# Six blocks of the projection phase made into one, and the next sequence's input and q weights requested at the head of the attention block

## The chip, the cores and the metric

The kernel runs on the 8 cores of one Trainium2 chip. Each core takes two of the 16 sequences and works on its own; no core waits for another. The time is device time in microseconds (us) of the slowest core. A profile is one execution, recorded on the slowest core, with the span and granted TensorE clock of all eight. PE is TensorE, DVE is VectorE, ACT is ScalarE, POOL is GpSimd, SP is SyncE.

## The reference, cut to what matters

One transformer layer over x of (16, 2048, 1024) in float32: attention, a LayerNorm, a feed-forward part with quantized activations and weights and a depthwise convolution, and a LayerNorm.

```
def _L0_attn_ref(x, w_qkv, w_fc, b_fc, gamma, beta):
    qkv = jnp.einsum('bsd,ed->bse', x, w_qkv)
    q, k, v = jnp.split(qkv, 3, axis=-1)
    att = jax.nn.softmax(jnp.einsum('bqd,bkd->bqk', q, k) * scaling, axis=-1)
    y = jnp.einsum('bqk,bvd->bqd', att, v)
    y = jnp.einsum('bqd,ed->bqe', y, w_fc) + b_fc
    h = x + y
    return layernorm(h) * gamma + beta
...
x = _layernorm(x + _L0_attn_ref(...))
x = _layernorm(x + _L0_ffn_ref(x, w1, conv_w, conv_b, w2))
```

The einsum 'bqk,bvd->bqd' sums att over k and v over its own positions, so that each row of y is the row sum of att times the sum of all rows of v. The kernel makes use of this: it needs q, k, the row sums of the softmax, and one row, the sum of x over the positions times the v weights times the fc weights.

## The kernel before

The program is a row of blocks. A helper class, PB, collects each engine's instructions and waits in lists; run() writes them out as one block, and the next block begins on every engine when all engines have ended the one before (the waits show such a block end as PEq L65). Inside a block each engine runs its own list in order, and semaphores order the engines among each other: mm counts PE's groups, vv DVE's, ssm ACT's, dG the DMAs of POOL, dS and dSb those of SP. After each of its DMA instructions POOL also runs a drain.

First come constants (P0) and the means of the feed-forward weights (W0), until 209 us. Then, for each of the two sequences:

- A0: POOL requests the feature-major input, eight DMAs of 128 x 2048 elements from float32 into the bfloat16 tile xf (L432), and the q weights, eight DMAs of 128 x 1024 elements into wbuf (wload, L411). It waits for all of them, and the block ends.
- A1: PE multiplies in 32 groups of eight matmuls (L445), alternating between two PSUM banks; DVE evicts each group into qf (L453).
- A2kl: POOL loads the k weights into the same wbuf, and the block ends when they are there.
- A2k: the same 32 groups with the k weights, evicted into kf (L469).
- A2v: DVE sums xf over the positions, eight reductions of 2048 elements (L479); PE multiplies the sums with the v weights, which SP brings in eight pieces through a buffer of two (L491, L497); the row goes to DRAM and back as columns (L508, L512).
- A2w: the same with the fc weights (L529, L535), and the row is spread to all partitions in wrowbc (L550).
- A3: sixteen query tiles. For each, SP loads a residual tile into xres (L581), PE forms 128 x 2048 scores in 32 matmuls (L589), DVE takes maxima (L598), ACT the exponentials and their sums (L607), and emit_epilogue adds, normalizes twice, quantizes and has ACT store x1, a scale, and the quantized tile (L291 to L398). The epilogue of a tile is emitted inside the next tile's turn. Of DVE's work over 1024 elements there, L330, L365, L384, L387, L393 and L627 read one tile each.
- A3drain: every engine waits for all stores and loads of A3.

The tile xf is allocated for A0 to A2v alone and is given back before A3; wbuf is allocated throughout. In A3 POOL has nothing to do, and neither xf nor wbuf is used.

After both sequences come the feed-forward half: w1 quantized, the first matmul with the convolution (F1), w2 quantized, and the second matmul (F2). Nothing of it is touched by the change.

Of the kernel before, what the change touches and what calls it, by code (L numbers as in the profile page):

```python
# [8 lines left out]
BF16 = mybir.dt.bfloat16  # L9
# [72 lines left out]
def build_program(cfg: Cfg, debug=False):  # L82
    nc = bass.Bass("TRN2", target_bir_lowering=False)
    S, D, H, DC, HC = cfg.S, cfg.D, cfg.H, cfg.DC, cfg.HC
    T, G, KB, KBW = cfg.T, cfg.G, cfg.KB, cfg.KBW
    T1, T2, ST = cfg.T1, cfg.T2, cfg.ST
    NGRP, NQT, NSEQ = cfg.NGRP, cfg.NQT, cfg.NSEQ
# [10 lines left out]
    x_fm = din("x_fm", (NSEQ, D, S))  # L98
    wqT = din("wqT", (D, D))
# [68 lines left out]
    dG = Sem(E(nc.semaphore("dG")))  # L168
    dO = Sem(E(nc.semaphore("dO")))
    mm = Sem(E(nc.semaphore("mm")))  # L170
    vv = Sem(E(nc.semaphore("vv")))
# [3 lines left out]
    p = PB(nc, "P0")  # L175
    for dst, srcd in ((ident, ident_d), (identf, identf_d), (esel, esel_d),
                      (onescol, ones_d), (c128, c128_d)):
        p.op("sync", lambda s, dst=dst, srcd=srcd: s.dma_start(
            out=dst[:], in_=srcd.ap()), inc=dS, k=16)
    p.op("sync", lambda s: s.dma_start(  # L180
        out=gammaBC[:], in_=_ap(gamma_d.tensor, 0, [[0, 128], [1, D]])),
        inc=dS, k=16)
    p.op("sync", lambda s: s.dma_start(
        out=betaBC[:], in_=_ap(beta_d.tensor, 0, [[0, 128], [1, D]])),
        inc=dS, k=16)
    p.op("sync", lambda s: s.dma_start(
        out=bfcBC[:], in_=_ap(bfc_d.tensor, 0, [[0, 128], [1, D]])),
        inc=dS, k=16)
    for c in range(HC):
        p.op("sync", lambda s, c=c: s.dma_start(  # L190
            out=cwcol[:, 3 * c:3 * c + 3], in_=cw_d[c * 128:(c + 1) * 128, :]),
            inc=dS, k=16)
    for c in range(HC):
        p.op("sync", lambda s, c=c: s.dma_start(
            out=cbcol[:, c:c + 1], in_=cb_d[c * 128:(c + 1) * 128, :]),
            inc=dS, k=16)
# [5 lines left out]
    with nc.sbuf_tensor("wstage", [128, H], F32) as wstage, \  # L202
         nc.sbuf_tensor("wstage2", [128, H], F32) as wstage2, \
         nc.sbuf_tensor("wabs", [128, H], F32) as wabs:
        p = PB(nc, "W0")
# [5 lines left out]
        for i, (src, width) in enumerate(chunks):  # L211
# [7 lines left out]
            if i >= 1:  # L219
                p.wait("scalar", vv, vv.n)  # L220
            p.op("scalar", lambda sc, stage=stage, width=width: sc.activation(
                out=wabs[:, 0:width], in_=stage[:, 0:width], func=AF.Abs), inc=ssm)
            p.wait("vector", ssm, ssm.n)
            p.op("vector", lambda v, i=i, width=width: v.reduce_sum(
                out=colsb[:, i:i + 1], in_=wabs[:, 0:width], axis=AX.X), inc=vv)
        p.op("vector", lambda v: v.reduce_sum(
            out=cols[:, 0:1], in_=colsb[:, 0:DC], axis=AX.X))
        p.op("vector", lambda v: v.reduce_sum(
            out=cols[:, 1:2], in_=colsb[:, DC:DC + HC], axis=AX.X), inc=vv)
# [8 lines left out]
            out=wsmat[0:1, 2:3], in0=wsmat[0:1, 0:1], scalar1=1.0 / (D * H),  # L238
            scalar2=1e-5, op0=ALU.mult, op1=ALU.max))
        p.op("vector", lambda v: v.tensor_scalar(  # L240
            out=wsmat[0:1, 3:4], in0=wsmat[0:1, 1:2], scalar1=1.0 / (D * H),
# [6 lines left out]
            out=wsmat[0:1, 8:9], in0=wsmat[0:1, 6:7], scalar1=-1.0, scalar2=None,  # L248
            op0=ALU.mult))
        p.op("vector", lambda v: v.tensor_scalar(  # L250
            out=wsmat[0:1, 9:10], in0=wsmat[0:1, 7:8], scalar1=-1.0, scalar2=None,
            op0=ALU.mult), inc=vv)
        p.wait("tensor", vv, vv.n)
        for j, cell in enumerate((4, 5, 8, 9)):
# [5 lines left out]
             inc=vv)  # L260
# [141 lines left out]
    attn_stack = ExitStack()  # L402
# [6 lines left out]
    def wload(p, src):  # L409
        for dc in range(DC):  # L410
            p.op("gpsimd", lambda g, dc=dc, src=src: g.dma_start(  # L411
                out=wbuf[:, dc * D:(dc + 1) * D],
                in_=src[dc * 128:(dc + 1) * 128, :]), inc=dG, k=16)

    def mm_evac(p, items, emit_group, emit_evac, banks):
# [3 lines left out]
        for i, it in enumerate(items):  # L419
# [5 lines left out]
            emit_evac(p, it, banks[i % nb])  # L425
            assert vv.n == evbase + i + 1

    for s_i in range(NSEQ):
        with nc.sbuf_tensor(f"xf{s_i}", [128, DC * S], BF16) as xf:
            p = PB(nc, f"A0_{s_i}")  # L430
            for dc in range(DC):
                p.op("gpsimd", lambda g, dc=dc: g.dma_start(  # L432
                    out=xf[:, dc * S:(dc + 1) * S],
                    in_=x_fm[s_i, dc * 128:(dc + 1) * 128, :]), inc=dG, k=16)
            wload(p, wqT)
            p.wait("gpsimd", dG, dG.n)
            p.run()

            q_items = [(cb, ec) for cb in range(S // KBW) for ec in range(DC)]

# [14 lines left out]
                    in0=bank[:, 0:KBW], scalar1=cfg.QSCALE, scalar2=None,  # L455
                    op0=ALU.mult), inc=vv)

            p = PB(nc, f"A1_{s_i}")
            mm_evac(p, q_items, q_group, q_evac, [ps_a, ps_b])
            p.run()  # L460

            p = PB(nc, f"A2kl_{s_i}")
            wload(p, wkT)
            p.wait("gpsimd", dG, dG.n)
            p.run()

            def k_evac(p, it, bank):
                cb, ec = it
# [1 line left out]
                    out=kf[:, ec * S + cb * KBW: ec * S + (cb + 1) * KBW],  # L470
                    in_=bank[:, 0:KBW]), inc=vv)

            p = PB(nc, f"A2k_{s_i}")
            mm_evac(p, q_items, q_group, k_evac, [ps_a, ps_b])
            p.run()

            p = PB(nc, f"A2v_{s_i}")
            for dc in range(DC):
                p.op("vector", lambda v, dc=dc: v.reduce_sum(  # L479
                    out=colsb[:, 32 + dc:33 + dc], in_=xf[:, dc * S:(dc + 1) * S],  # L480
# [5 lines left out]
            for dc in range(DC):  # L486
                sem = dS if dc % 2 == 0 else dSb
                if dc >= 2:
# [3 lines left out]
                    out=wf32[:, (dc % 2) * D:(dc % 2 + 1) * D],  # L492
                    in_=wvT[dc * 128:(dc + 1) * 128, :]), inc=sem, k=16)
# [8 lines left out]
            for h in range(NDH):  # L502
                bank = ps_c if h == 0 else ps_d
                p.op("vector", lambda v, h=h, bank=bank: v.tensor_copy(
                    out=vrow[0:1, h * DH:(h + 1) * DH], in_=bank[0:1, 0:DH]),
                    inc=(vv if h == NDH - 1 else None))
            p.wait("sync", vv, vv.n)
            p.op("sync", lambda s: s.dma_start(out=vrow_d, in_=vrow[0:1, :]),  # L508
                 inc=dS, k=16)
            p.wait("sync", dS, dS.n)  # L510
            for dc in range(DC):
                p.op("sync", lambda s, dc=dc: s.dma_start(  # L512
                    out=colsb[:, 40 + dc:41 + dc],
                    in_=_ap(vrow_d.tensor, dc * 128, [[1, 128], [1, 1]])),
                    inc=dS, k=16)
            p.run()

        p = PB(nc, f"A2w_{s_i}")
        p.wait("sync", dS, dS.n)
        p.wait("sync", dSb, dSb.n)  # L520
        p.wait("tensor", dS, dS.n)
# [2 lines left out]
        for dc in range(DC):  # L524
            sem = dS if dc % 2 == 0 else dSb
            if dc >= 2:
# [3 lines left out]
                out=wf32[:, (dc % 2) * D:(dc % 2 + 1) * D],  # L530
                in_=wfcT[dc * 128:(dc + 1) * 128, :]), inc=sem, k=16)
# [7 lines left out]
        for h in range(NDH):  # L539
# [3 lines left out]
                out=rowbuf[0:1, 0:DH], in_=bank[0:1, 0:DH]), inc=vv)  # L543
# [7 lines left out]
                out=wrowbc[:, h * DH:(h + 1) * DH], in_=ps_s[0][:, 0:DH]),  # L551
                inc=vv)
# [15 lines left out]
        if True:  # L568
            if True:
                p = PB(nc, f"A3_{s_i}")  # L570
                dO_bases = {0: dO.n, 1: dOb.n}
                exp_ev = {}
                mm_at = {}
                epi_q = {}
                for qt in range(NGRP * NQT):
# [3 lines left out]
                    if qt >= 2:  # L579
                        p.wait("sync", vv, ev_h2_list[qt - 2])  # L580
                    p.op("sync", lambda s, row0=row0, qt=qt: s.dma_start(  # L581
                        out=xres[:, (qt % 2) * D:(qt % 2 + 1) * D],
                        in_=x_tm[row0:row0 + 128, :]), inc=ldsem, k=16)
# [579 lines left out]
```

How the kernel before makes its waits and increments, by code:

```python
        def cl(e, fn=fn, tgt=tgt, drain=drain):  # L52
            ins = fn(e)
            if tgt is not None:
                ins.then_inc(*tgt)
            if drain:
                e.drain()
# [3 lines left out]
    def wait(self, eng, sem, val):  # L61
        self.items[eng].append(lambda e, h=sem.h, v=val: e.wait_ge(h, v))
```

## Time and profile before

| | us |
|---|---|
| median of 2 runs | 4921.29 (4916.14 and 4926.43) |
| the profiled execution | 4925.33 |
| its span, slowest core (core 1) | 4923.6 |
| spans of the other cores | 4901.7 to 4923.3 |
| A0 to A2w, first sequence | 209 to 522 |
| A3 and drain, first sequence | 522 to 997 |
| A0 to A2w, second sequence | 997 to 1313 |
| A3 and drain, second sequence | 1313 to 1784 |
| feed-forward half | 1784 to 4923 |

The span runs from the first to the last instruction of a core; the time of an execution has a little around it. Busy time of an engine is the time in which it executes; DMA instructions of POOL are counted as busy while they are issued (about 0.5 us each), the transfers themselves are not. A row of the order of time gives the start and the length in us, the engine, the line, what is written and read, how many instructions are merged, and in brackets how long the engine was idle before and what ended that.

### The profile page before, as it was taken

The page shows a single profiled execution, that of the slowest core. Times are in us where ns is not written, and L with a number is a line of the kernel's source. Part 1 is how long each engine was busy: PE and PEld are TensorE (multiplying, and loading weights), DVE is VectorE, ACT ScalarE, POOL GpSimd, SP SyncE. Part 2 cuts the span into 40 slices and gives each one's busy share as a digit, 9 for nine tenths or more (in the row PEclk, how much of TensorE's full clock was granted, in tenths as well). Part 3 has the DMA queues.
Part 4 walks back from the last instruction along what each step waited for, and adds up shares of the span by engine and source line. Part 5 has one row for each costly group of instructions (what it writes and reads, how often), then busy time and mean ns, then how long its engine had stood idle before and what let it go on. Part 6 is the DMA issues. An engine that isn't in the chain of part 4 may idle for free. (4 is left out here: it accounts for less than half of the span.)

```text
span 4923.6 us, 35107 instructions; the slowest of 8 cores (4901.7 to 4923.6 us)
## 1 busy us (share of the span) xinstructions
PE 1830.1 (37%) x8500; PEld 922.5 (19%) x8500; DVE 3281.7 (67%) x4522; ACT 967.7 (20%) x1773; POOL 25.7 (1%) x52
## 2 busy tenths in 40 slices
PE   0046533127533303423323323233333333106999
PEld 0022111013111102211212211122111121003444
DVE  3313488802388876888888888888888888874333
ACT  2200122100022202222223222232222322100111
POOL 0000000000000000000000000000000000000000
PEclk9998766658766656666566666566565766558999
DMA  5521111131211131000000000000000000035543
GB/s 165 150 36 46 58 52 45 45 51 18 77 54 43 53 131 38 1 23 23 23 23 16 7 24 23 23 13 11 23 23 24 21 3 18 17 120 166 163 145 107
DMA packets 189264, 258.95 MB, mean 53 GB/s; under 512 B 63490, under 2 KB 131330, under 8 KB 187012
## 3 DMA queue, kind: packets, MB, share of 16 engines
q1 hardware_dynamic: 163716, 197.95, 13.4%
q10 hardware_dynamic: 18432, 41.97, 2.2%
q0 software_dynamic: 6912, 16.78, 2.1%
q14 instruction: 134, 1.10, 0.1%
q8 instruction: 70, 1.15, 0.1%
HBM read 188.47 MB, written 75.52 MB: 54 GB/s over the span
## 5 line engine op out<-in xcount | busy, mean ns | idle before, releaser
L868 PE MATMUL ps_a<-xqF,tw 128*128 128x258 bf16 (+1 forms) x1024 | 219.3, 386 | 1002.5 <-DVE ubuf L879 777.0
L892 ACT ACTIVATE vt<-ubuf,cbcol,cwcol 128x256 f32<-128x256 f32 x512 | 307.7, 601 | 919.2 <-DVE ubuf L879 889.0
L589 PE MATMUL ps_s<-kf,qf 128*128 128x512 bf16 x1024 | 294.9, 459 | 507.9 <-ACT disc L607 505.6
L868 PE MATMUL ps_s<-xqF,tw 128*128 128x258 bf16 (+1 forms) x2048 | 315.2, 308 | 50.5 <-DVE ubuf L879 47.6
L868 PEld LDWEIGHTS ps_a<-xqF,tw 128*128 128x128 bf16 x1024 | 124.9, 130 | 1080.4 <-issue 1037.9
L816 DVE TENSOR_TENSOR accb<-accb,rbuf 128x2048 bf16<-128x2048 bf16 x256 | 313.6, 1225 | 19.7 <-issue 0.9
L756 DVE SCALAR_TENSOR_TENSOR vt<-ubuf,cwcol,vt 128x256 f32<-128x256 f32 x512 | 248.3, 485 | 84.5 <-issue 55.2
L763 DVE SCALAR_TENSOR_TENSOR vt<-ubuf,cwcol,vt 128x256 f32<-128x256 f32 x512 | 248.3, 485 | 40.4 <-issue 2.6
L1031 PE MATMUL ps_c<-tw,hq 128*128 128x512 bf16 x512 | 195.4, 382 | 200.9 <-DMA hq<-hqs 200.9
L771 ACT ACTIVATE ubuf<-vt 128x256 f32<-128x256 f32 x512 | 213.7, 417 | 269.6 <-DVE vt L763 252.7
L915 PE MATMUL ps_c<-identf,maxM 128*128 128x128 f32 x64 | 19.1, 454 | 644.3 <-DVE maxM L908 644.3
L908 DVE TENSOR_REDUCE maxM<-ubuf 128x256 f32<-128x8192 f32 x16 | 247.5, 15467 | 9.9 <-ACT ubuf L771 9.9
L794 ACT ACTIVATE iqq<-zscr,c 128x2048 int32<-128x2048 f32 x64 | 128.1, 2002 | 604.1 <-DVE zscr L783 604.1
L589 PEld LDWEIGHTS ps_s<-kf,qf 128*128 128x128 bf16 x1024 | 114.6, 114 | 688.9 <-issue 615.6
L445 PE MATMUL ps_a<-xf,wbuf 128*128 128x512 bf16 x512 | 127.7, 395 | 302.8 <-PEq L65 302.8
L868 PEld LDWEIGHTS ps_s<-xqF,tw 128*128 128x128 bf16 x2048 | 209.6, 109 | 161.7 <-issue 114.7
L868 PE MATMUL ps_b<-xqF,tw 128*128 128x258 bf16 (+1 forms) x1024 | 216.3, 383 | 10.3 <-DVE ubuf L879 8.7
L1040 PE MATMUL ps_d<-tw,hq 128*128 128x512 bf16 x512 | 195.3, 381 | 0.0
L1031 PE MATMUL ps_s<-tw,hq 128*128 128x512 bf16 x512 | 194.0, 379 | 0.0
L1040 PE MATMUL ps_s<-tw,hq 128*128 128x512 bf16 x512 | 194.0, 379 | 0.0
L813 DVE TENSOR_SCALAR rbuf<-dsb 128x2048 bf16<-128x2048 bf16 x256 | 177.7, 694 | 20.0 <-issue 0.4
L607 ACT ACTIVATE disc<-ps_s,colsb 128x512 f32<-128x512 f32 x128 | 88.0, 687 | 409.0 <-DVE colsb L601 402.3
(137 smaller groups left out, 3041.0 us busy)
## 6 DMA issues: line engine op xcount, KB each, us to landing
hqs<-hqst SPq DMA_DIRECT2D x16, 2048.0 KB, 8.9
wstage<-w1T SPq DMA_DIRECT2D x8, 2048.0 KB, 10.3
wstage<-w2T SPq DMA_DIRECT2D x32, 512.0 KB, 4.0
xres<-x_tm SPq DMA_DIRECT2D x32, 512.0 KB, 3.4
x1s<-x1t ACTq DMA_DIRECT2D x32, 512.0 KB, 5.7
qstage<-w1T SPq DMA_DIRECT2D x8, 2048.0 KB, 8.7
qstage<-w2T SPq DMA_DIRECT2D x32, 512.0 KB, 3.3
xres<-x1s SPq DMA_DIRECT2D x32, 512.0 KB, 8.1
```

What stands on the lines that cost most here:

```text
L589: t.matmul(ps_s[kb][:, 0:KBW], qf[:, dc * S + qcol: dc * S + qcol + 128], kf[:, dc * S + kb * KBW: dc * S + (kb + 1) * KBW], start=(dc == ...
L756: v.scalar_tensor_tensor(out=vt2[:, cpar * T1W2:cpar * T1W2 + T1], in0=ubuf[:, hc * T1W2:hc * T1W2 + T1], scalar=cwcol[:, 3 * hc:3 * hc + ...
L763: v.scalar_tensor_tensor(out=vt1[:, cq * T1W2:cq * T1W2 + T1], in0=ubuf[:, hc * T1W2 + 2:hc * T1W2 + 2 + T1], scalar=cwcol[:, 3 * hc + 2:3 ...
L771: p.op("scalar", lambda sc, hc=hc, cq=cq: sc.activation(out=ubuf[:, hc * T1W2 + 1:hc * T1W2 + 1 + T1], in_=vt1[:, cq * T1W2:cq * T1W2 + T1 ...
L794: p.op("scalar", lambda sc, FD=FD: sc.activation(out=iqq[:, 0:FD], in_=zscr[:, 0:FD], func=AF.Identity, bias=c128[:, 0:1], scale=1.0), inc ...
L813: p.op("vector", lambda v, FD=FD, thr=thr: v.tensor_scalar(out=rbuf[:, 0:FD], in0=dsb[:, 0:FD], scalar1=thr, scalar2=None, op0=ALU.is_ge))
L816: p.op("vector", lambda v, FD=FD: v.tensor_tensor(out=accb[:, 0:FD], in0=accb[:, 0:FD], in1=rbuf[:, 0:FD], op=ALU.add))
L868: lo=lo, hi=hi, w0=w0, W=W: t.matmul(bank[:, 0:W], tw[:, dc * H + hc * 128: dc * H + hc * 128 + 128], xqF[:, (par * DC + dc) * WW + (lo - w0):
L892: p.op("scalar", lambda sc, hc=hc: sc.activation(out=vt1[:, (hc % 4) * T1W2:(hc % 4) * T1W2 + T1], in_=ubuf[:, hc * T1W2 + 1:hc * T1W2 + 1 ...
L908: p.op("vector", lambda v: v.reduce_max(out=maxM[:, 0:T1], in_=_ap(ubuf, 1, [[HC * T1W2, 128], [1, T1], [T1W2, HC]]), axis=AX.X, apply_abs ...
L1031: banks=banks: t.matmul(banks[0][:, 0:DH], hq2[:, slot + hc * T1 + sq * 128: slot + hc * T1 + sq * 128 + 128], tw[:, hc * D + 0:hc * D + D ...
L1040: banks=banks: t.matmul(banks[1][:, 0:DH], hq2[:, slot + hc * T1 + sq * 128: slot + hc * T1 + sq * 128 + 128], tw[:, hc * D + DH:hc * D + ...
```

## The change

- xf becomes one tile for both sequences, allocated for the whole attention half.
- The sixteen DMA instructions of A0 move into a function, emit_A0, which remembers the semaphore's count in dGq. For sequence 0 it is called at the head of the projection block; for sequence 1 it is called at the head of A3 of sequence 0.
- A0, A1, A2kl, A2k, A2v and A2w, six blocks, become one, APRO. In place of the five block ends between them stand waits: POOL and PE wait for the load of A0 (dGq), POOL waits for the last q matmul before it loads the k weights, and PE waits for these and for the last q eviction.

```
--- before.py
+++ after.py
@@ -425,16 +425,24 @@
             emit_evac(p, it, banks[i % nb])
             assert vv.n == evbase + i + 1
 
+    xf = attn_stack.enter_context(nc.sbuf_tensor("xfb", [128, DC * S], BF16))
+    dGq = {}
+
+    def emit_A0(p, s_i):
+        for dc in range(DC):
+            p.op("gpsimd", lambda g, dc=dc, s_i=s_i: g.dma_start(
+                out=xf[:, dc * S:(dc + 1) * S],
+                in_=x_fm[s_i, dc * 128:(dc + 1) * 128, :]), inc=dG, k=16)
+        wload(p, wqT)
+        dGq[s_i] = dG.n
+
     for s_i in range(NSEQ):
-        with nc.sbuf_tensor(f"xf{s_i}", [128, DC * S], BF16) as xf:
-            p = PB(nc, f"A0_{s_i}")
-            for dc in range(DC):
-                p.op("gpsimd", lambda g, dc=dc: g.dma_start(
-                    out=xf[:, dc * S:(dc + 1) * S],
-                    in_=x_fm[s_i, dc * 128:(dc + 1) * 128, :]), inc=dG, k=16)
-            wload(p, wqT)
-            p.wait("gpsimd", dG, dG.n)
-            p.run()
+        if True:
+            p = PB(nc, f"APRO_{s_i}")
+            if s_i not in dGq:
+                emit_A0(p, s_i)
+            p.wait("gpsimd", dG, dGq[s_i])
+            p.wait("tensor", dG, dGq[s_i])
 
             q_items = [(cb, ec) for cb in range(S // KBW) for ec in range(DC)]
 
@@ -455,14 +463,12 @@
                     in0=bank[:, 0:KBW], scalar1=cfg.QSCALE, scalar2=None,
                     op0=ALU.mult), inc=vv)
 
-            p = PB(nc, f"A1_{s_i}")
             mm_evac(p, q_items, q_group, q_evac, [ps_a, ps_b])
-            p.run()
-
-            p = PB(nc, f"A2kl_{s_i}")
+
+            p.wait("gpsimd", mm, mm.n)
             wload(p, wkT)
-            p.wait("gpsimd", dG, dG.n)
-            p.run()
+            p.wait("tensor", dG, dG.n)
+            p.wait("tensor", vv, vv.n)
 
             def k_evac(p, it, bank):
                 cb, ec = it
@@ -470,11 +476,8 @@
                     out=kf[:, ec * S + cb * KBW: ec * S + (cb + 1) * KBW],
                     in_=bank[:, 0:KBW]), inc=vv)
 
-            p = PB(nc, f"A2k_{s_i}")
             mm_evac(p, q_items, q_group, k_evac, [ps_a, ps_b])
-            p.run()
-
-            p = PB(nc, f"A2v_{s_i}")
+
             for dc in range(DC):
                 p.op("vector", lambda v, dc=dc: v.reduce_sum(
                     out=colsb[:, 32 + dc:33 + dc], in_=xf[:, dc * S:(dc + 1) * S],
@@ -513,9 +516,7 @@
                     out=colsb[:, 40 + dc:41 + dc],
                     in_=_ap(vrow_d.tensor, dc * 128, [[1, 128], [1, 1]])),
                     inc=dS, k=16)
-            p.run()
-
-        p = PB(nc, f"A2w_{s_i}")
+
         p.wait("sync", dS, dS.n)
         p.wait("sync", dSb, dSb.n)
         p.wait("tensor", dS, dS.n)
@@ -568,6 +569,8 @@
         if True:
             if True:
                 p = PB(nc, f"A3_{s_i}")
+                if s_i + 1 < NSEQ:
+                    emit_A0(p, s_i + 1)
                 dO_bases = {0: dO.n, 1: dOb.n}
                 exp_ev = {}
                 mm_at = {}
```

## Rows read from the trace of the kernel before

**Rows 1.** the page, busy time of each engine and DVE over 40 slices

```profile
PE 1830.1 (37%) x8500; PEld 922.5 (19%) x8500; DVE 3281.7 (67%) x4522; ACT 967.7 (20%) x1773; POOL 25.7 (1%) x52
...
DVE  3313488802388876888888888888888888874333
```

**Rows 2.** spans and granted clock of the two slowest cores

```profile
core 1: 4923.6 us, clock 0.696
...
core 6: 4923.3 us, clock 0.701
```

**Rows 3.** core 1 by stretch: length, busy (count) by engine, clock, DMA

```profile
209.00:287.00 78.00, 0.22 (x1) 0.14 (x2) 0.00 (x0) 0.00 (x0) 8.58 (x16) 1.00 0.49 81
...
438.00:522.00 84.00, 37.28 (x69) 5.75 (x70) 22.39 (x14) 0.00 (x0) 0.00 (x0) 0.77 0.32 100
522.00:997.00 475.00, 150.44 (x512) 58.03 (x512) 355.42 (x576) 100.89 (x257) 0.00 (x0) 0.63 0.13 45
997.00:1079.00 82.00, 0.27 (x1) 0.14 (x2) 0.00 (x0) 0.00 (x0) 8.45 (x16) 0.50 0.48 77
```

**Rows 4.** order of time, core 1, first A3 to second A1

```profile
983.14 0.34 ACTq L398 DMA_DIRECT2D xqs<-xqt  x1
997.17 0.53 POOL L432 DMA_DIRECT2D xf<-x_fm  x1 [621.75 <-PEq L65]
...
1074.78 0.53 POOL L411 DMA_DIRECT2D wbuf<-wqT  x1 [3.59 <-issue]
...
1078.73 3.57 PE L445 MATMUL ps_a<-xf,wbuf 128*128 128x512 bf16 x8 [156.48 <-PEq L65]
```

**Rows 5.** the same two points on core 6

```profile
997.75 0.53 POOL L432 DMA_DIRECT2D xf<-x_fm  x1 [617.59 <-PEq L65]
...
1077.90 3.52 PE L445 MATMUL ps_a<-xf,wbuf 128*128 128x512 bf16 x8 [154.95 <-PEq L65]
```

**Rows 6.** order of time, core 1, block ends, first sequence

```profile
282.76 0.53 POOL L411 DMA_DIRECT2D wbuf<-wqT  x1 [3.46 <-issue]
...
286.78 0.58 PE L445 MATMUL ps_a<-xf,wbuf 128*128 128x512 bf16 x1 [78.57 <-PEq L65]
...
343.07 1.89 PE L445 MATMUL ps_b<-xf,wbuf 128*128 128x512 bf16 x8
...
346.52 0.53 POOL L411 DMA_DIRECT2D wbuf<-wkT  x1 [63.23 <-PEq L65]
...
374.89 0.53 POOL L411 DMA_DIRECT2D wbuf<-wkT  x1 [3.55 <-issue]
...
378.83 3.57 PE L445 MATMUL ps_a<-xf,wbuf 128*128 128x512 bf16 x8 [33.87 <-PEq L65]
...
437.17 0.69 DVE L469 CAST kf<-ps_b 128x512 bf16<-128x512 f32 x1 [1.03 <-PE ps_b L445]
438.25 4.64 DVE L479 TENSOR_REDUCE colsb<-xf 128x1 f32<-128x2048 bf16 x2 [0.39 <-PEq L65]
```

**Rows 7.** SyncE's own waits, first 2600 us: total, times, longest

```profile
SPq L62 <- DMA colsb<-vrow_d: 3.4, 2, 2.1
```

**Rows 8.** DMA issues and queue share while the second load runs

```profile
q0 software_dynamic: 2304, 6.29, 47.8%
...
xf<-x_fm POOLq DMA_DIRECT2D x8, 512.0 KB, 5.7
wbuf<-wqT POOLq DMA_DIRECT2D x8, 256.0 KB, 3.5
```

**Rows 9.** DMA issues in the first A3, the residual load

```profile
xres<-x_tm SPq DMA_DIRECT2D x16, 512.0 KB, 3.4
```

**Rows 10.** groups of instructions, core 1, 560 to 960 us, two of DVE's six

```profile
L330 DVE TENSOR_SCALAR ln1t<-atile,cols 128x1024 f32<-128x1024 f32 x15 | 12.2, 813 | 10.1 <-ACT cols L315 10.1
...
L627 DVE TENSOR_SCALAR atile<-wrowbc,colsb 128x1024 f32<-128x1024 f32 x14 | 10.5, 753 | 1.1
```

**Rows 11.** waits of core 1, 560 to 960 us: total, times, longest

```profile
DVE x1t L365 <- ACT cols L359: 11.1, 15, 0.7
```

## The prediction

> **What bounds the kernel now.** I read the page first. VectorE (DVE) is busy for 67% of the span and TensorE (PE) for 37% [rows 1], but the average hides stages in which neither works. The line of forty slices shows them: DVE falls to 1 in the third slice and to 0 and 2 in the ninth and tenth (a slice is 123 us). So the next view is the table by stretch for core 1 [rows 3]. From 209 to 287 us, and again from 997 to 1079 us, PE is busy for less than 0.3 us, DVE and ScalarE for nothing; the only work is sixteen GpSimd (POOL) DMA instructions, with the DMA engines 48 to 49% busy. These are the blocks A0_0 and A0_1, which fetch the feature-major input and the q weights of a sequence. Between them lies A3_0, 522 to 997 us: DVE 355 of 475 us busy, POOL idle, DMA engines 13% busy. DVE sets the pace there: its own waits are short (0.7 us at the longest before L365 [rows 11]), and PE needs only 150 of the 475 us. The chain of work through the attention half is therefore load, q projection, load, k projection, a serial piece (438 to 522 us), A3, and the same again; what lies on it counts in full, because each block ends when all its engines have ended.
>
> The order of time puts the edges on it [rows 4]. The first A3 issues its last store at 983.14; a drain block waits for it; POOL issues the first transfer of the second load at 997.17, the last of its sixteen at 1074.78, and PE starts the second q projection at 1078.73. The second load costs core 1 1078.73 − 997.17 = 81.6 us.
>
> **The change, part by part.**
>
> *The second load moves into A3_0.* Removed from the path: 81.6 us on core 1 and 1077.90 − 997.75 = 80.15 us on core 6 [rows 5]. The time is that of the slowest core, and these two stand at 4923.6 and 4923.3 us [rows 2], so what counts is 4923.6 − 81.6 = 4842.0 and 4923.3 − 80.15 = 4843.15: core 6 becomes the slower, and the gain of this part is 4923.6 − 4843.15 = 80.45 us. The drain block before it stays, and so does the wait of 14 us for the last store.
>
> All sixteen DMA instructions move. They stand at the head of POOL's queue in A3_0, which has no other work, and wait for nothing: the readers of the input tile and of the weights ended before the previous block did. SyncE's and ScalarE's queues are not touched. The cover is 475 us for 81.6 us of loading, a factor of 5.8. The load runs at the start of A3_0, beside about 81.6 / 475 × 16 = 2.75, so three, query tiles.
>
> What it takes from them: first, DMA. The load uses 47.8% of the sixteen engines [rows 8] and A3 uses 13% [rows 3]; the sum is 61%. A residual tile lands in 3.4 us now [rows 9] and is issued about a tile (475 / 16 = 29.7 us) ahead of its use; even if a whole 5.7 us transfer of the load stood before it [rows 8], it would be in time. Cost nothing; without that lead it would be 5.7 us for each of three tiles. Second, DVE and POOL at the same time, which no stretch of before shows: wherever POOL works, DVE is idle. Per tile DVE has six instructions over 1024 elements that run in 0.7 to 0.8 us, more than one element in each nanosecond (L330, L365, L384, L387, L393, L627; two of them in [rows 10]). If POOL can hold something that these need, the bound from below is nothing, since each kind may pass untouched, and a gain is excluded because they do the same work. The bound from above is one POOL instruction of 0.53 us [rows 4] for each of 6 × 3 = 18 instructions, 9.5 us. I take 1 us, near the lower end, because POOL is busy for 8.5 of the 82 us [rows 3], about a tenth of the time, and a tenth of 9.5 us is 1.
>
> In the other direction those six instructions fill about 6 × 0.75 = 4.5 us of a 29.7 us tile, 15%. Were POOL locked out for all of them, the load would need 81.6 / 0.85 = 96 us instead of 81.6, still far inside 475. The Trainium skill (SBUF — State Buffer, "Summary: rules for kernel authors") warns against exactly such an overlap: descriptor generation for GpSimd's DMAs is starved while DVE runs its two-port modes, and it would have these DMAs issued from another queue. Its example, about 620 ns alone against 3100 ns overlapped, is a factor of 5; an estimate by it is a load of 5 × 81.6 = 408 us, which A3_0 would still cover. No run here shows that yet.
>
> *Six blocks of a sequence become one.* Where the blocks ended [rows 6], first sequence: the last q matmul ends at 343.07 + 1.89 = 344.96 and POOL starts the k weights at 346.52, a gap of 1.56 us which held the last eviction and the block's end. Now POOL waits for the matmul alone; I leave 0.3 us for the semaphore and take 1.26. The last k weight is issued at 374.89 and lands after 3.5 us (the row of the same transfers in [rows 8]), at 378.39; PE starts at 378.83: 0.44, of which 0.4 saved. The last k eviction ends at 437.86 and the row sums start at 438.25: 0.39, of which 0.32 saved. The q projection starts at 286.78, its last weight lands at 282.76 + 3.5 = 286.26: 0.4 saved, in the first sequence only (in the second that block's end went with the load). The end of A2v saves nothing: SyncE waits there 1.7 us each time for the column transfers to land [rows 7], and it still does. Sum: 2.38 in the first sequence and 1.98 in the second, 4.4 us. The bounds are 0 (other waits take it all) and twice that, 8.8.
>
> *What stays.* The k weights are still loaded behind the last q matmul, since both use one buffer. POOL's wait has only those eight DMAs behind it, and PE waits for them: 378.83 − 346.52 = 32.3 us of idle PE per sequence is not touched. PE's added wait for the evictions is over long before.
>
> *What comes early.* In the one block SyncE's first two loads of the v weights are issued at its start, beside the first input transfers in the first sequence. They are 512 KB each, like a residual tile's 3.4 us. The bound is 6.8 us, below is nothing; the load's transfers leave the DMA engines half idle [rows 3], so I take 1 us. In the second sequence they run beside matmuls, at no cost.
>
> *Sum.* 80.45 + 4.4 − 1 − 1 = 82.85 us. The profiled execution took 4925.3 us, 1.7 more than its span; the median of the runs is 4921.3, 4.0 below it. So 4925.3 − 82.85 = 4842.5 by the profiled execution, and 4838.5 by the median: 1.7% less. Within 2% (4822.9 to 5019.7 us), about what a measurement of this kernel can tell from no change, this counts as the same.
>
> **The rivals.**
>
> *DVE is held up by the load.* For: nothing in the trace excludes it. Against: POOL's short busy time. At the upper bound above, 8.5 us more than I took: 4847 us.
>
> *The load outlasts A3_0.* POOL's transfers would have to take over 5.8 times as long; at a factor of 7, 571 − 475 = 96 us would be left, and PE would start as late as before: 4838.5 + 80.45, about 4919 us, or with a few us less than 96, in between. Against: the six instructions fill only 15% of a tile.
>
> *Slower than before: POOL and DVE block each other through all of A3_0.* If the load is stretched over the whole stage, all 6 × 16 = 96 such DVE instructions meet it, and each may wait for POOL. From 82.85 / 96 = 0.86 us each the gain is gone; at 1.0 us, 4838.5 + 96 = 4934 us. Over 2% slower needs (82.85 + 98.4) / 96 = 1.9 us each. Against: 0.86 us is more than a whole POOL instruction.
>
> *More than the sum.* For over 2% faster the change must bring 98.4 us, 15.6 more than the sum. The block ends would have to hold four and a half times the 4.4 us that I read. The rows exclude it for this core; only another core or run could.
>
> *It does not do what it says.* If the load in A3_0 had to wait for something until the stage ends, 4.4 us would remain: about 4918 us. I see no such wait.
>
> **How the numbers follow.** The forecast has 0.76, with its own range of 4830 to 4846: 4.4 us more from block ends below, 5.8 us of early v loads above, and 2 to 4 us for other executions. DVE held up has 0.13, the load outlasting the stage 0.02, slower than before 0.02, more than the sum 0.04, no effect 0.03. The range is 4826 to 4852: it takes in the forecast and the first rival with 5 us around them, since the two times of before lie 10 us apart, and leaves out the other four, 0.11. Over 2% faster: 0.04. Over 2% slower: 0.01, half of the slower rival. Within 2%: 0.95.
>
> **What would show it.** In the profile after, POOL's sixteen instructions should stand within about 100 us from the start of A3_0, and the second q projection should start within 1 us of the drain's end. A3_0 should stay 475 us long, to 1 or 2 us; L330 and L627 should keep 813 and 753 ns. If A3_0 is longer by near 10 us, DVE was held up, and these two lines tell it. If POOL's transfers stand 20 us apart or more, it was starved. If the gap from the last q matmul to POOL is still 1.5 us, the block ends cost nothing. The forecast is wrong if another core had a much shorter second load than core 6 and a span near 4923, or if A3_0 pays for the load in a way that no row of before shows.

## The result

| | before | after |
|---|---|---|
| median of all executions, us | 4944.46 (10) | 4868.71 (12) |
| lowest, us | 4916.14 | 4830.39 |
| ratio | 1 | 0.9832, interval [0.9785, 0.988] |
| profiled execution, us | 4925.33 | 4868.29 |

The change takes 1.7% off the time, the share that the prediction gave (4838.5 / 4921.3 = 0.983); the interval reaches to both sides of 2%. The median of 4868.71 us lies 17 us above the range, though, and so does the first profiled execution. Executions of both kernels differ in the TensorE clock that is granted to pairs of cores (0 and 1, 2 and 3, and so on), and the ratio and its interval leave out those in which this makes one die over 1% slower. In two later series the changed kernel's median was 4863.67 (4 executions) and 4847.13 (6), beside 4931.56 and 4929.44 for the kernel before.

The spans and granted clocks of all cores of two profiled executions of the changed kernel, the first (4868.3 us) and one of the second series (4842.0 us):

```profile
core 0: 4839.6 us, clock 0.704
...
core 2: 4866.8 us, clock 0.696
core 3: 4862.2 us, clock 0.697
...
core 6: 4823.5 us, clock 0.706
...
core 0: 4830.5 us, clock 0.708
...
core 2: 4835.8 us, clock 0.705
core 3: 4840.5 us, clock 0.704
...
core 6: 4827.1 us, clock 0.705
```

In the first, cores 2 and 3 are 27 and 23 us later than core 0; their granted clock is 0.696 and 0.697 where that of the others is 0.703 or more. In the second no core stands out. The second is the one to hold against [rows 2]. Its page, busy time and the line of slices:

```profile
PE 1823.0 (38%) x8500; PEld 920.6 (19%) x8500; DVE 3281.8 (68%) x4522; ACT 967.6 (20%) x1773; POOL 26.1 (1%) x52
...
DVE  3313488823588767888888888888888888873334
```

Beside [rows 1] the counts of instructions are the same and the busy times of PE and DVE differ by 0.4% at most, and the second hole is narrower: DVE's ninth to eleventh slices were 0, 2 and 3 and are now 2, 3 and 5, and what is left of it are the projections and the serial piece, in which DVE has little to do. Order of time of core 3 there, from the last store of the first A3 to the second q projection (compare [rows 4]):

```profile
982.54 0.34 ACTq L398 DMA_DIRECT2D xqs<-xqt  x1
...
993.27 0.80 SPq L494 DMA_DIRECT2D wf<-wvT  x2
...
993.36 3.57 PE L453 MATMUL ps_a<-xfb,wbuf 128*128 128x512 bf16 x8 [71.75 <-PEq L65]
```

PE starts 10.8 us after the last store is issued, where it was 95.6 us on core 1 before (1078.73 − 983.14); the store lands at 992.57, so what is left is the drain's wait for it and the block ends.

Where the time went, stretch by stretch: means over the eight cores, read from the order of time of each core of the profiled executions, in us. The columns are two executions of the kernel before and two of the changed one.

| stretch | before | before, again | after | after, again | predicted difference |
|---|---|---|---|---|---|
| first load's start to first q eviction | 81.3 | 82.2 | 83.6 | 84.2 | +1 − 0.4 |
| its last weight landed to first q matmul (in the row above) | 0.50 | 0.50 | 0.14 | 0.14 | −0.4 |
| last q eviction's start to first k weight, first sequence | 1.45 | 1.45 | 0.43 | 0.43 | −1.26 |
| last k weight landed to first k matmul, first sequence | 0.51 | 0.51 | 0.25 | 0.25 | −0.4 |
| last k eviction's end to row sums | 0.38 | 0.38 | 0.09 | 0.09 | −0.32 |
| A3_0, DVE's first maximum to its last tile | 450.4 | 450.6 | 450.6 | 450.3 | +1 |
| A3_0's last tile to second q eviction | 94.8 | 94.1 | 13.5 | 12.9 | −80.45 |
| second load's first to sixteenth transfer | 75.5 | 75.6 | 110.1 | 115.6 | hidden |

From the start of the first load to the end of the second A3's last tile the cores take 1556.0 and 1555.6 us before and 1473.0 us after, again: 82.8 us less. (In the first execution of the changed kernel it is 1477.3 us; cores 0 and 1 had a lower clock in the second projections, as shown below.)

### The profile page after: what moved, and what is told of

It is laid out like the page before. It is cut to its first block and busy times, and to the rows that moved or that the text cites. A ratio compares the mean times of both kernels' runs of the same rounds, so it can differ in the third digit from the quotient of the medians.

```text
span 4866.8 us, 35003 instructions; the slowest of 8 cores (4823.5 to 4866.8 us)
## 1 busy us (share of the span) xinstructions
PE 1856.7 (38%) x8500; PEld 928.4 (19%) x8500; DVE 3281.8 (67%) x4522; ACT 967.6 (20%) x1773; POOL 25.8 (1%) x52
## 5 line engine op out<-in xcount | busy, mean ns | idle before, releaser
L871 PE MATMUL ps_s<-xqF,tw 128*128 128x258 bf16 (+1 forms) x2048 | 315.2, 308 | 55.4 <-DVE ubuf L882 52.7
L759 DVE SCALAR_TENSOR_TENSOR vt<-ubuf,cwcol,vt 128x256 f32<-128x256 f32 x512 | 248.3, 485 | 84.2 <-issue 55.2
L453 PE MATMUL ps_a<-xfb,wbuf 128*128 128x512 bf16 x512 | 127.4, 394 | 220.8 <-DMA wbuf<-wqT 80.7
L1043 PE MATMUL ps_s<-tw,hq 128*128 128x512 bf16 x512 | 202.6, 396 | 0.0
L1034 PE MATMUL ps_s<-tw,hq 128*128 128x512 bf16 x512 | 202.6, 396 | 0.0
```

The lines of the kernel that those rows point to most:

```text
L759: v.scalar_tensor_tensor(out=vt2[:, cpar * T1W2:cpar * T1W2 + T1], in0=ubuf[:, hc * T1W2:hc * T1W2 + T1], scalar=cwcol[:, 3 * hc:3 * hc + ...
L871: lo=lo, hi=hi, w0=w0, W=W: t.matmul(bank[:, 0:W], tw[:, dc * H + hc * 128: dc * H + hc * 128 + 128], xqF[:, (par * DC + dc) * WW + (lo - w0):
L1034: banks=banks: t.matmul(banks[0][:, 0:DH], hq2[:, slot + hc * T1 + sq * 128: slot + hc * T1 + sq * 128 + 128], tw[:, hc * D + 0:hc * D + D ...
L1043: banks=banks: t.matmul(banks[1][:, 0:DH], hq2[:, slot + hc * T1 + sq * 128: slot + hc * T1 + sq * 128 + 128], tw[:, hc * D + DH:hc * D + ...
```

## The experiments

### The kernels once more

No edit. Each execution comes with the clock and span of every core.

> The kernel before, unchanged, against itself. It is there for the executions: each lists its time and the granted clock of every core. Theory (the lower clock comes with or without the change): the ratio to the kernel before is 1.00 within 0.5%, and of its executions some stand near 4916 to 4926 us and others 35 to 60 us above these, the latter with one pair of cores whose mean granted clock is lower by 0.005 or more. Rival (the change itself brings the lower clock): all its executions stand within 10 us of 4920.

Measured: ratio to the kernel before 0.9995 [0.995, 1.004]. Six of its ten executions were at 4925 to 4961 us and four at 4989 to 5012; beside them the same kernel ran 19 times, eleven times at 4920 to 4934 and eight times at 4972 to 5009. In one at 4980.5, cores 2 and 3 had a clock of 0.683 and 0.687 and spans of 4978.8 and 4974.3, and all others stood at 4924 or less. So the kernel before has such executions too. The theory had them 35 to 60 us above the others; they stand up to 90 us above.

> The changed kernel once more, unchanged. Theory: its undisturbed executions stand at 4830 to 4843 us, and the others 25 to 50 us above, as often as those of the kernel before do; from the start of the first load to the last tile of the second A3 a core with full clock takes 1468 to 1478 us (1553 to 1563 before). Rival (the change brings the lower clock): more than half of its executions stand above 4855 us while those of the kernel before stand at 4920.

Measured: ratio 0.9834 [0.9762, 0.9905]; four executions, at 4842.0, 4844.2, 4883.2 and 4927.9 us, the last further up than the 25 to 50 us of the theory. In the profiled one, from the first load to the second A3's last tile the cores take 1468.3 to 1479.5 us.

> The changed kernel once more, for more executions of it and of the kernel before in turns. Theory (the lower clock comes with or without the change): executions of the changed kernel within 20 us of 4842 and executions well above it appear in both kernels at rates that can't be told apart (so far 25 of 55 of the kernel before stand over 30 us above its lowest, 10 of 16 of the changed one more than 15 us above 4842). Rival (the change brings it): at least four in five of the changed kernel's executions stand above 4860.

Measured: ratio 0.985 [0.9804, 0.9896]; six executions, four of them at 4838.7 to 4849.8, one at 4865.3 and one at 4892.6; the kernel before beside them seven times at 4921 to 4939 and four times at 4953 to 5001. In all, 12 of 22 executions of the changed kernel stand above 4855 us and 31 of 66 of the kernel before above 4935, each 15 us over its usual 4840 or 4920. The rival of four in five would need more than that; that the change has no part in it at all is not shown by such counts. The medians of a few executions hang on it: one pair of cores in a lower clock is enough, because the slowest core sets the time.

Where the first profiled execution lost its time, by stretch of the second matmul stage (F2), four rows of core 2 and then four of core 0: busy time (instructions) of PE, PEld, DVE, ACT and POOL, then granted clock, DMA share and GB/s:

```profile
4400.00:4500.00 100.00, 100.00 (x465) 45.33 (x464) 41.32 (x67) 12.66 (x30) 0.00 (x0) 1.00 0.43 138
4500.00:4600.00 100.00, 100.00 (x465) 45.30 (x463) 40.28 (x69) 11.96 (x32) 0.00 (x0) 1.00 0.49 159
4600.00:4700.00 100.00, 100.00 (x427) 43.57 (x426) 35.02 (x58) 9.33 (x24) 0.00 (x0) 0.91 0.42 135
4700.00:4800.00 100.00, 100.00 (x382) 41.44 (x381) 31.83 (x55) 9.33 (x24) 0.00 (x0) 0.81 0.40 129
...
4400.00:4500.00 100.00, 99.53 (x456) 45.32 (x464) 39.69 (x66) 12.17 (x29) 0.00 (x0) 1.00 0.42 138
4500.00:4600.00 100.00, 99.53 (x456) 45.30 (x463) 40.98 (x68) 12.04 (x30) 0.00 (x0) 1.00 0.51 163
4600.00:4700.00 100.00, 99.53 (x456) 45.36 (x464) 39.07 (x65) 11.30 (x30) 0.00 (x0) 1.00 0.46 149
4700.00:4800.00 100.00, 99.47 (x455) 45.33 (x464) 38.09 (x63) 10.89 (x28) 0.00 (x0) 1.00 0.40 136
```

PE is busy throughout on both cores. On core 2 the mean granted clock falls from 1.00, the 2.4 GHz level, to 0.91 and 0.81 while PE runs on without a pause, and it does 427 and 382 matmuls in 100 us, where it did 465. On core 0 the clock stays at 1.00. F2 took core 2 482.6 us from its first matmul to the end of its span and core 1 454.8 us: 28 us, and 4866.8 is 27 us above the next pair's 4839.6. The Trainium skill (TensorE: Matmul & The Clock Gate, "Seeing it yourself") names a peak-current limiter that grants 13/16 of the clock, which is 0.81, to a whole die. The value agrees with these rows; its reach does not in this execution, since cores 0 and 1 of the same die keep 1.00, and in the execution of 4842.0 us core 3 runs the same stage at 1.00 with all eight cores at work.

The same level shows on another pair in another stage. Core 1 of the same execution, in the first and in the second q projection:

```profile
283.00:336.00 53.00, 53.00 (x245) 23.97 (x244) 21.45 (x31) 0.00 (x0) 0.00 (x0) 1.00 0.00 1
990.00:1035.00 45.00, 45.00 (x173) 18.67 (x172) 15.01 (x22) 0.00 (x0) 0.00 (x0) 0.81 0.00 1
```

There it cost over 10 us in each of the second sequence's two projections (65.2 and 66.1 us from the first eviction to the last, in place of 54.7 and 55.4 in the first sequence), but cores 0 and 1 ended ahead of the slowest all the same.

The profile of the kernel before has this level too. Its core 6, in the first A3, while PE works on one query tile, with the columns as above:

```profile
590.00:600.00 10.00, 5.52 (x22) 2.07 (x19) 8.08 (x16) 1.55 (x4) 0.00 (x0) 0.81 0.31 105
```

It costs nothing there, since DVE sets the pace of A3. The other profiled executions with a late pair agree: in the run with the second load alone cores 0 and 1 have 0.81 in F2 and cores 2 and 3 in the first projections, in the run with the late v weights cores 6 and 7 have it in F2. The executions that were not profiled show only each core's mean clock and span.

### The second load alone

```
+            if s_i == 0:
+                emit_A0(p, s_i)
             p.wait("gpsimd", dG, dG.n)
             p.run()
 ...
                 p = PB(nc, f"A3_{s_i}")
+                if s_i + 1 < NSEQ:
+                    emit_A0(p, s_i + 1)
```

> The second load alone moves to the head of A3_0 into one common input tile; the six blocks of a sequence stay. Theory: it brings all of the large part: from A3's last tile to the first q eviction about 14 us in place of about 95, so 80 us less; the first load keeps its 81.3 us, since the v weights are requested late as before; 4920 - 80 = 4840 us, the same as the whole change within 3 us, as the block ends (3.4 us less) and the slower first load (2.3 us more) cancel in it. Rival (the blocks made into one carry part of the gain beyond their ends): 4850 us or more.

Measured: ratio 0.9872 [0.9791, 0.9954], lowest execution 4845.2 us. From the last tile to the q eviction 15.1 us on a mean over the cores, the first load 82.1 us. The four executions are at 4845.2, 4873.0, 4908.3 and 4927.3 us; in the profiled one (4873.0) cores 0 to 3 had the lower clock. The lowest stands 3 us above the changed kernel's 4842.0 of the same series, less than executions differ by. The load alone carries nearly all of the gain.

### The blocks made into one, alone

```
                 p = PB(nc, f"A3_{s_i}")
-                if s_i + 1 < NSEQ:
-                    emit_A0(p, s_i + 1)
```

> The six blocks of a sequence become one, but the second load stays at the head of the second projection block. Theory: 1.0 us less from the last q eviction to the first k weight, 0.3 us less from the last k eviction to the row sums, 0.35 us less from the last weight to the matmuls, each twice, and 2.3 us more for each of the two loads, since the first v weights are then requested beside them: between 1 us more and 1 us less, about 4920 us. The prediction's price for this part was 4.4 us less at the block ends and 1 us more: 4917. Rival (block ends are worth more than the profile shows): 4910 or less.

Measured: ratio 0.9996 [0.9945, 1.0047], lowest 4924.7 us. The block ends give what the table shows (0.43 for 1.45 us, 0.09 for 0.38, and 0.25 for 0.51 us from the last weight to the matmuls), and the first load takes 84.7 us. This part of the change moves nothing that can be measured in the time of an execution: what the ends give, the early v weights take.

### The v weights as late as before

```
             mm_evac(p, q_items, q_group, k_evac, [ps_a, ps_b])
+            p.wait("sync", mm, mm.n)
```

> The changed kernel with one wait more: SyncE requests the first v weights only when the last k matmul has ended, as before the change. Theory (the early v weights take DMA time from the first load): from the first load's first transfer to the first q eviction 81.5 us on a mean over the cores, as in the kernel before, in place of 84.2. Rival (the one block itself slows the load): it stays at 84.

Measured: 82.3 us, against 84.2, 83.6 and 84.7 in three executions with the early request, and 81.3 and 82.2 in two of the kernel before. SyncE's two transfers of 512 KB cost the first load about 2 us, and not the block. (Its one execution, 4902.3 us, had cores 6 and 7 at a mean clock of 0.693 and 0.695 and says nothing of the time.)

### The load four times

```
                 if s_i + 1 < NSEQ:
-                    emit_A0(p, s_i + 1)
+                    for _rep in range(4):
+                        p.wait("gpsimd", dG, dG.n)
+                        emit_A0(p, s_i + 1)
```

> The changed kernel with the second load issued four times in A3_0, each time after the one before has landed, so that POOL's DMAs run beside nearly all of A3_0's tiles. Theory (DVE is not held up): the four loads take 4 x 113 = 450 us, end just inside A3_0, and from DVE's first maximum to its last tile A3_0 stays at 450 to 451.5 us. Rival 1 (DVE is held up a little by each transfer): A3_0 is longer by 2 us or more. Rival 2 (the load can outlast the stage): from A3's last tile to the first q eviction the time grows from 13 us to 30 us or more.

Measured, one execution, 4931.3 us. A3_0 took 450.6 us on a mean, so DVE is not held up, with POOL's transfers beside every one of its tiles. But the four loads took 539 to 556 us, first to last, and did not fit. Order of time of POOL on core 0, and PE's start:

```profile
528.22 0.53 POOL L433 DMA_DIRECT2D xfb<-x_fm  x1 [145.62 <-POOLq L65]
...
652.99 0.53 POOL L411 DMA_DIRECT2D wbuf<-wqT  x1 [4.12 <-issue]
659.72 0.53 POOL L433 DMA_DIRECT2D xfb<-x_fm  x1 [6.20 <-DMA wbuf<-wqT]
677.33 0.53 POOL L433 DMA_DIRECT2D xfb<-x_fm  x1 [17.07 <-issue]
...
1083.72 0.53 POOL L411 DMA_DIRECT2D wbuf<-wqT  x1 [3.67 <-issue]
...
1088.75 3.57 PE L453 MATMUL ps_a<-xfb,wbuf 128*128 128x512 bf16 x8 [161.49 <-PEq L65]
```

From its first to its sixteenth transfer the first load took 125 us on this core, from 528.22 to 652.99, the second and third 178 and 160, over twice the 75.5 us alone, and the fourth, which ran on past the stage, 75. PE waited for it until 1088.75, 98 us on a mean over the cores from the last tile to the q eviction: rival 2 as stated. The theory's 113 us for each load came from a load whose first transfers run before the first tile's stores. A3_0 covers fewer than three such loads and not the 5.8 that I had from the load's length alone.

### Small stores in A3

```
-                out=x1s[row0:row0 + 128, :], in_=x1), inc=sto, k=16)
+                out=x1s[row0:row0 + R, :], in_=x1[0:R, :]), inc=sto, k=16)
```

and the same for f1s and xqs, with R = 1 in the first sequence.

> The changed kernel with the three stores of each tile of the first A3 cut to one partition of 128 (all rows are filled in an extra block behind A3, so the first sequence's result is not the reference's). It asks why the load takes 113 us beside A3 and 76 us alone. Theory A (POOL's transfers stand behind ScalarE's stores in the DMA engines): with the small stores the sixteen transfers take 80 us or less, first to last. Theory B (DVE's fast instructions keep POOL from issuing): still 100 us or more, with gaps of over 10 us.

Measured: 78.6 to 80.9 us on the eight cores, against 104 to 123 us in the changed kernel. Order of time of POOL, first the changed kernel (core 3), then this one (core 0):

```profile
524.20 0.53 POOL L433 DMA_DIRECT2D xfb<-x_fm  x1 [145.12 <-POOLq L65]
...
567.17 0.99 POOL L433 DMA_DIRECT2D xfb<-x_fm  x1 [5.01 <-issue]
580.92 0.53 POOL L411 DMA_DIRECT2D wbuf<-wqT  x1 [12.76 <-issue]
591.97 0.53 POOL L411 DMA_DIRECT2D wbuf<-wqT  x1 [10.52 <-issue]
...
616.76 0.53 POOL L411 DMA_DIRECT2D wbuf<-wqT  x1 [18.87 <-issue]
...
647.43 0.53 POOL L411 DMA_DIRECT2D wbuf<-wqT  x1 [3.77 <-issue]
...
520.45 0.53 POOL L434 DMA_DIRECT2D xfb<-x_fm  x1 [145.19 <-POOLq L65]
...
563.56 0.53 POOL L434 DMA_DIRECT2D xfb<-x_fm  x1 [5.13 <-issue]
569.95 0.53 POOL L412 DMA_DIRECT2D wbuf<-wqT  x1 [5.86 <-issue]
574.15 0.53 POOL L412 DMA_DIRECT2D wbuf<-wqT  x1 [3.68 <-issue]
...
599.89 0.53 POOL L412 DMA_DIRECT2D wbuf<-wqT  x1 [3.50 <-issue]
```

Until the first tile's stores both go at 5.6 us a transfer. From then on the changed kernel has four gaps of 10.5 to 18.9 us, and the kernel with small stores has none, though DVE does the same work in both. So the load is slow because of ScalarE's stores, as theory A has it, and DVE's fast instructions alone have next to no part in it: 79.6 us beside them, 75.5 us alone. The edit cut three stores of each tile at once, x1s of 512 KB, f1s of 0.5 KB and xqs of 256 KB, so it does not tell which of them does it, nor whether they would do it without DVE's work beside them.

Below, before (core 1) and after (core 3), in each tile x1s is issued first, f1s 2.3 us later and xqs 5 us after that. The 0.5 KB of f1s take 8.6 us to land before and 16.3 us after, and x1s goes from 2.8 to 10.6 us. The stores are not the same on every core, though: on core 3 before, x1s takes 10.3 us without any load beside it. The residual loads of SyncE land in 3.2 us, but they are issued when the last tile's stores have landed, and say nothing of how a load fares beside them.

```profile
x1s<-x1t ACTq DMA_DIRECT2D x14, 512.0 KB, 2.8
xqs<-xqt ACTq DMA_DIRECT2D x14, 256.0 KB, 12.0
f1s<-cols ACTq DMA_DIRECT2D x14, 0.5 KB, 8.6
...
wbuf<-wqT POOLq DMA_DIRECT2D x8, 256.0 KB, 5.6
xres<-x_tm SPq DMA_DIRECT2D x3, 512.0 KB, 3.2
x1s<-x1t ACTq DMA_DIRECT2D x3, 512.0 KB, 10.6
xqs<-xqt ACTq DMA_DIRECT2D x4, 256.0 KB, 14.0
f1s<-cols ACTq DMA_DIRECT2D x4, 0.5 KB, 16.3
```

### The k weights early

```
+        wload(p, wkT, wbufk, dK)      # behind the q weights, in emit_A0
...
-            p.wait("gpsimd", mm, mm.n)
-            wload(p, wkT)
-            p.wait("tensor", dG, dG.n)
+            p.wait("tensor", dK, dKn)
```

> The changed kernel with a second weight buffer: the k weights are requested behind the q weights, in the first projection block and in A3_0, and PE goes from the q to the k groups without a stop. Theory: 33 us from the last q matmul to the first k matmul go, and 2.4 us of the k projection's slow start, in each sequence: 71 us less than the changed kernel, 4771 us where the granted clock is full; A3_0 as long as before, since 24 transfers need 170 us of its 450. Rival (24 transfers hold DVE up or outlast the stage): over 4785 us.

Measured: ratio 0.9689 [0.9619, 0.9758], four executions at 4775.3, 4777.9, 4790.1 and 4812.0 us. From the first q to the last k eviction the cores take 110.6 to 111.7 us in place of 146, in each sequence (only cores 6 and 7, at a lower granted clock, 125 and 126 us in the first): 35 us less, twice, as stated. Two executions stand above the rival's 4785 us, but not for the rival's reasons: A3_0 stays at 450.7 us and the load ends inside it, with 12.6 us from the last tile to the q eviction. PE on core 2 goes from the q to the k weights with a gap of 0.95 us:

```profile
343.88 1.89 PE L462 MATMUL ps_b<-xfb,wbuf 128*128 128x512 bf16 x8
...
346.72 1.89 PE L462 MATMUL ps_a<-xfb,wbufk 128*128 128x512 bf16 x8 [0.95 <-DVE qf L470]
```

### The first load early too

```
         p = PB(nc, "W0")
+        emit_A0(p, 0)
```

> The kernel with the early k weights, and the first load of 24 transfers moved too, to the head of block W0, which reads all feed-forward weights for their means in 205 us with the DMA engines about half busy. Theory: the 84 us between W0 and the first q eviction shrink to 4; POOL's 16 MB and W0's 32 MB share the DMA engines, 48% and 55% busy alone, so that W0 grows by what does not fit, 10 to 35 us: 45 to 70 us less than the kernel with the early k weights, 4705 to 4730 us where the granted clock is full, over 4% less than the kernel before. Rival (W0 is bound by its DMAs and pays for the load in full): W0 grows by 80 us and nothing is gained, 4775 us.

Measured: ratio 0.9545 [0.9471, 0.9618], five executions at 4704.2, 4711.3, 4732.3, 4734.3 and 4800.7 us. The first q eviction starts 4.4 us after W0's last instruction (below, core 0). On a mean over the cores W0's last instruction starts at 225.4 us, 19 us later than in the changed kernel, and the first q eviction starts at 229.8 us in place of 291.3: 61.5 us less. W0 pays for a part of the load, as stated. In the profiled execution (4734.3) cores 0 and 1 had 0.81 of the clock in the first projections and cores 2 and 3 in F2. This is the fastest version of the study.

```profile
222.53 0.16 DVE L285 COPY wqcols<-ps_d 128x4 f32<-128x4 f32 x1 [2.09 <-PE ps_d L281]
226.92 0.69 DVE L471 TENSOR_SCALAR qf<-ps_a 128x512 bf16<-128x512 f32 x1 [4.22 <-PE ps_a L463]
```

## Why the prediction was right and wrong

**The second load (80.45 us) was right.** 94.8 and 94.1 us became 13.5 and 12.9: 81.2 to 81.3 us less on a mean over the cores, and the experiment with the load alone shows that it is this part.

**DVE held up (1 us, bound 9.5)** was nothing: A3_0 stays within 0.3 us. Its instructions in the stage, by the groups of 560 to 960 us (compare [rows 10]), keep 813 and 753 ns. The load ends near 650 us, so most of these ran without it; the last two rows are from core 0 of the run with four loads, where POOL's transfers stand beside all of them:

```profile
L330 DVE TENSOR_SCALAR ln1t<-atile,cols 128x1024 f32<-128x1024 f32 x14 | 11.4, 813 | 9.4 <-ACT cols L315 9.4
...
L630 DVE TENSOR_SCALAR atile<-wrowbc,colsb 128x1024 f32<-128x1024 f32 x14 | 10.5, 753 | 1.1
...
L330 DVE TENSOR_SCALAR ln1t<-atile,cols 128x1024 f32<-128x1024 f32 x15 | 12.2, 813 | 10.1 <-ACT cols L315 10.1
...
L632 DVE TENSOR_SCALAR atile<-wrowbc,colsb 128x1024 f32<-128x1024 f32 x14 | 10.5, 753 | 1.1
```

Of the other four kinds the mean over all cores grows by 2 ns at most in that run, and single instructions by up to 0.1 us. In the other direction, the one POOL instruction of 0.99 us in place of 0.53 in the rows above, at 567.17, runs while DVE's L365 does.

**The block ends (4.4 us)** gave 1.02 + 0.26 + 0.30 us in each sequence and 0.36 us at the first q projection, 3.5 us. From the last q matmul's end to POOL's first DMA 0.54 us are left, where I had 0.3 for the semaphore, and from the last k weight to PE 0.25, where I had 0.04.

**The early v weights (1 us)** cost 1.9 us by the run that requests them late (82.3 for 84.2), and 2.5 by the table (81.8 before, 83.9 after, of which 0.36 is the block end that no longer stands there).

Together 81.3 + 3.5 − 2.5 = 82.3 us, or 82.9 with 1.9 for the v weights; measured in one piece, below the table, it is 82.8, against 82.85 in the sum. That it agrees so closely is partly luck: the large term came out 0.8 us too small and DVE's 1 us was not needed, and against these stand the block ends, 0.9 us too large, and the v weights, 0.9 to 1.5 us too small. Ten of the changed kernel's 22 executions stand at 4830.4 to 4849.8 us, around the 4842.5 that the sum gave for the profiled one, and the ratio is the one forecast.

**The range was wrong,** and with it the time as a number: 4868.71 us lies above 4852. The step that failed is the last one, where the two times of the kernel before, 10 us apart, stood for what executions differ by, "2 to 4 us for other executions" and "5 us around them". Neither of the two was one of the late ones; that was luck, since 31 of 66 executions of the kernel before are late. The runs show 4830 to 4929 us for the changed kernel and 4916 to 5012 us for the one before; in about half of the executions one or more pairs of cores are later by 20 to 90 us, and in each of those whose traces were read the pair ran a part of F2 or of the projections at 0.81 of the clock. The profile before had both halves of this: the level of 0.81, on core 6 in A3, and in F2 a stage of 454 us with PE busy throughout. At 0.81 of the clock all of such a stage would take 454 / 0.81 = 560 us, 106 more, an estimate of the most that F2 can lose. What puts a pair at that level in one execution and not in another stays open. The ratio to the kernel before, run in turns, came out as forecast; the time given alone did not.

**The cover of the load** was argued wrongly, though it did not matter. I had 61% of the DMA engines' time taken, three tiles beside the load, and DVE's fast instructions as the only thing that could slow POOL. ScalarE's stores, which I left out, slow it. The load takes 110 to 116 us beside A3, half as long again as alone (75.5), and 150 to 180 us when all of it runs beside stores; A3_0 covers fewer than three loads in a row, not 5.8. The factor of 5 for starved descriptor generation, which I had from the Trainium skill (SBUF — State Buffer, "A bandwidth-pool intuition that's wrong (but worth ruling out)"; the warning itself stands in "Summary: rules for kernel authors"), does not show here: with the stores small, the load beside DVE's work takes 79.6 / 75.5 = 1.05 times what it takes alone.

**The rivals.** The load that outlasts A3_0 came true only when it was issued four times, and it then costs what was worked out for it: the q projection started as late as before. More than the sum, no effect and slower than before all fell with the table above.

## What to carry to other kernels

A load that stands alone between two stages is worth its full length when it is moved under a stage whose engines leave its queue idle; price it on the slowest cores, and look for the buffer that keeps its neighbour from going the same way: the second weight buffer brought 35 us in each sequence, nearly as much again, for 16 KB a partition. Block ends are worth 0.3 to 1 us each in this kernel, and making blocks into one also lets other queues start early, which cost nearly as much here. When a time is given as a number and not as a ratio, its range must hold what executions of the same kernel differ by, and two executions don't show that. Read the granted clock of every core in the profile before, also where it costs nothing: a level that shows up on one pair can meet the stage that TensorE bounds in the next execution.

## What the runs showed of the hardware

- The granted clock has a level of 0.81 besides 1.00 and 0.50, for pairs of cores and single stages of an execution, while PE is busy without a pause. A matmul stage runs 18% fewer matmuls in it (382 in 100 us for 465).
- ScalarE's three stores of a tile (512, 0.5 and 256 KB) hold up POOL's transfers by up to 19 us: sixteen take 110 to 116 us beside them and 79.6 us when the stores are cut to one partition. Which store does it was not separated.
- A store of 128 x 1 elements, 0.5 KB, took 8.6 us to land before (core 1) and 16.3 us beside POOL's load (core 3), where SyncE's loads of 512 KB take 3.2 us.
- Transfers of POOL beside a DVE that is busy 75% of the time left the mean of DVE's six instructions of 0.7 to 0.8 us as they were, to 2 ns, also where they ran beside all of the stage.
